# An attention and FFN kernel: batch 0's maximum spread by halves, first scores moved ahead of group 1's transposes, FFN constants made on Pool

## The reference

```python
ig = (ifg @ igate_w.T + igate_b).T          # ifg = [q, k, v] side by side
log_f = jax.nn.log_sigmoid(ifg @ fgate_w.T + fgate_b).T
cs = jnp.cumsum(log_f, axis=1)
log_D = where(tril, cs[:, :, None] - cs[:, None, :], -inf) + ig[:, None, :]
max_log_D = jnp.max(log_D, axis=-1, keepdims=True)
C = (qk / sqrt(16)) * exp(log_D - max_log_D)
h = (C / (maximum(abs(C.sum(-1)), exp(-max_log_D)) + 1e-6)) @ v
x = x + layernorm(h) * ln_scale
```

## Time and profile before

| | |
|---|---|
| median of 3 runs | 128.93 us (128.54 to 129.97) |
| profiled execution: its own time | 127.34 us |
| profiled execution: span | 125.6 us |
| PE matmuls, busy share of the span | 84% |
| DVE | 82% |
| ACT | 62% |
| POOL | 49% |
| mean granted TensorE clock | 0.973 of full |

### The profile page before, as it was taken

The page is one execution under the profiler, slowest core; times in us unless marked ns, Lnnn a source line. Parts: engine busy times, 40 slices in busy tenths (PEclk is TensorE's granted clock), DMA queues, the critical chain, the costliest instruction groups (busy, mean ns, idle before and its releaser), DMA issues.

```text
span 125.6 us, 3302 instructions
## 1 busy us (share of the span) xinstructions
PE 105.5 (84%) x1087; PEld 74.8 (60%) x1087; DVE 103.0 (82%) x347; ACT 78.1 (62%) x226; POOL 62.1 (49%) x137
## 2 busy tenths in 40 slices
PE   4889797928974578999979999999999999898950
PEld 4777793513451234468655866766866767696940
DVE  5459968999969999983999799999899999847331
ACT  4012939982984969478867996988897342525110
POOL 6835040527687857845363665864751554520000
PEclk9999999999999955999999999999999999999999
DMA  2995134982873259600311990100100100110101
GB/s 69 257 242 123 32 65 163 240 198 94 300 281 67 45 198 266 211 0 3 55 31 44 343 337 14 44 5 0 42 0 0 47 0 0 52 42 0 42 5 42
DMA packets 13537, 12.56 MB, mean 100 GB/s; under 512 B 2112, under 2 KB 11728, under 8 KB 13520
## 3 DMA queue, kind: packets, MB, share of 16 engines
q1 hardware_dynamic: 12384, 12.00, 33.2%
q10 hardware_dynamic: 1136, 0.35, 1.1%
HBM read 9.99 MB, written 1.31 MB: 90 GB/s over the span
## 4 chain that ended last, share of the span: by engine, by line
POOL 37%; issue 27%; PE 10%; DMA 8%; DVE 7%; ACT 4%; SPq 4%; POOLq 1%; DVEq 0%; ACTq 0%
POOL maxb L941 9%; POOL rs_x L910 7%; POOL rs_h L910 6%; PE pF L438 6%; POOL x2p L960 5%; SPq L292 4%; DMA xs<-in_x 3%; DMA maxb<-running_max 3%; POOL ve_x L909 2%; POOL ve_h L909 2%; PE pF L417 2%; POOL vals L931 2%; DMA running_max<-max_row 2%; POOL rs_q L920 2%; ACT dmat L550 2%
## 5 line engine op out<-in xcount | busy, mean ns | idle before, releaser
L550 ACT ACTIVATE dmat<-maxb,aT 128x128 f32<-128x128 f32 x128 | 39.2, 391 | 0.4 <-DVE maxb L685 0.4
L438 PE MATMUL pF<-h,w 128*128 128x256 f16 x256 | 30.3, 273 | 0.0
L438 PEld LDWEIGHTS pF<-h,w 128*128 128x128 f16 x256 | 24.7, 98 | 2.6
L790 DVE SCALAR_TENSOR_TENSOR h<-pF,h 128x512 f16<-128x512 f32 x32 | 20.9, 679 | 5.9 <-ACT h L573 5.9
L573 ACT ACTIVATE h<-pF 128x512 f16<-128x512 f32 x32 | 18.0, 591 | 9.8 <-PE pF L438 9.8
L368 PE MATMUL pS<-q_heads,qcT 64*128 64x512 f32 x64 | 20.4, 662 | 1.8 <-DVE cmat L696 1.8
L696 DVE SCALAR_TENSOR_TENSOR cmat<-pS,dmat 128x512 f32<-128x512 f32 x32 | 20.4, 680 | 0.5 <-PE pS L368 0.3
L960 POOL TENSOR_TENSOR x2p<-x,x2p 128x128 f16<-128x128 f32 x16 | 6.8, 427 | 25.3 <-ACT x2p L565 25.3
L941 POOL TENSOR_SCALAR_AFFINE_SELECT maxb<-maxb 128x1024 f32<-128x1024 f32 x14 | 15.4, 1102 | 6.4 <-DMA maxb<-running_max 6.4
L380 PEld LDWEIGHTS pO<-cmat,vals 128*32 128x32 f32 x256 | 6.4, 112 | 11.1 <-issue 9.0
L380 PE MATMUL pO<-cmat,vals 128*32 128x128 f32 x256 | 10.7, 287 | 1.8 <-POOL vals L931 0.9
(11 more groups left out here) (93 smaller groups left out, 170.2 us busy)
## 6 DMA issues: line engine op xcount, KB each, us to landing
maxb<-running_max SPq DMA_DIRECT2D x14, 512.0 KB, 5.9
xs<-in_x SPq DMA_DIRECT2D x4, 256.0 KB, 5.4
q_heads<-qcT SPq DMA_DIRECT2D x32, 32.0 KB, 2.2
out<-outb SPq DMA_DIRECT2D x8, 128.0 KB, 1.8
cs_in<-in_ctx SPq DMA_DIRECT2D x3, 256.0 KB, 6.8
cs_in<-in_ctx ACTq DMA_DIRECT2D x1, 256.0 KB, 4.5
k_in<-in_L_ffn_k SPq DMA_DIRECT2D x1, 256.0 KB, 5.6
running_max<-max_row SPq DMA_DIRECT2D x4, 64.0 KB, 1.7
```

The source lines that it names most:

```text
L438: last = pe.matmul(bank[:, u], w1[:, k, columns], h1[:, k, part], start=(k == 0 and part == 0), stop=(k == FT - 1 and part == 1))
L550: last = act.activation(dmat[:, n % 2, h], maxb[:, g % 2, j, h], ACT.Exp, bias=aT[:, g % 2, j, h:h + 1], scale=-1.0)
L790: dve.scalar_tensor_tensor(out=hidden(f, m, 1), in0=ffn_place(f, m), scalar=0.0, in1=hidden(f, m, 0), op0=ALU.max, op1=ALU.subtract).then_ ...
```

## The change

- `spread_max` and `direct_mask` work by half batches, with a semaphore count for each half, and batch 1's halves go to a third FFN bank and to `pO`, no longer to `pS`. ACT's `decay` of batches 0 and 1 waits for its own half. `scores(0)` no longer waits for the masks.
- PE: `scores(0)` now stands ahead of `turn(1, 1)` and `turn(1, 0)`.
- ACT: both halves of `decay(0)` stand ahead of `turn_out(1, 1)`. `gate_out` signals after each of its reads, and the addition of EPS (`em_guard`) is a function of its own behind `turn_out(1, 0)`.
- `ffn_scalars` goes from DVE to Pool, between `q_scale(0, 4)` and `q_scale(4, 4)`. `ffn_weights_0_2` goes to Pool too, behind `take_values(1)` and a wait for `m_ready`; it has four instructions there instead of three, through a new tile.
- DVE: the four half masks stand ahead of `q_group(2)`; in slot 0 `norm_group(2)` stands ahead of `forget_min(1)`, and `gate_scans(1)` stands behind `make_c(1)` in slot 1.

The diff, without the two functions removed from DVE, which are the same but for w0 (there `w0 = k0_in[0] - k0_in[1]`, then times the scale in place):

```diff
@@ -122,6 +122,7 @@
         k0_in = sb("k0_in", [128, 2, F], U8)
         k1_in = sb("k1_in", [128, FT, F], U8)
         k2_in = sb("k2_in", [128, FT, D], U8)
+        w0_half = sb("w0_half", [128, 2, F], F16)
         w0 = sb("w0", [128, F], F16)
         w1 = sb("w1", [128, FT, F], F16)
         w2 = sb("w2", [128, FT, D], F16)
@@ -205,6 +206,8 @@
         max_ready = sem("max_ready")
         m_ready = sem("m_ready")
         am_turned = sem("am_turned")
+        aT_ready = sem("aT_ready")
+        am_taken = sem("am_taken")
         am_ready = sem("am_ready")
         max_stored = sem("max_stored")
         max_spread = [[sem(f"max_spread{p}{j}") for j in range(GB)] for p in range(2)]
@@ -248,9 +251,9 @@
 
         def direct_place(i, half):
 
-            if i == 1:
-                return pS[:, 4 * half:4 * half + 4]
-            return pF[half][:, :].rearrange("p a (h s) -> p (a h) s", s=S)
+            if (i, half) == (1, 1):
+                return pO[:, :]
+            return pF[2 * i + half][:, :].rearrange("p a (h s) -> p (a h) s", s=S)
 
         def hidden(f, m, part):
 
@@ -320,7 +323,7 @@
                 if part == 1:
                     pe.wait_ge(ctx_loaded[g], 16)
                     if g >= 1:
-                        pe.wait_ge(am_ready, g)
+                        pe.wait_ge(am_taken, g)
                 else:
                     pe.wait_ge(xn_ready, GB * (g + 1))
                     pe.wait_ge(turned_out, 2 * g + 1)
@@ -344,14 +347,13 @@
                 pe.transpose(pG[:, 2], a_row[:, :], ident[:, :])
                 pe.transpose(pG[:, 3], m_row[:, :], ident[:, :]).then_inc(am_turned, 1)
 
-            def spread_max(i):
-
+            def spread_max(i, half):
 
                 g, j = divmod(DIRECT[i], GB)
                 pe.wait_ge(max_ready, g + 1)
-                for h in range(NH):
+                for h in range(4 * half, 4 * half + 4):
                     row = 32 * j + h
-                    last = pe.matmul(direct_place(i, h // 4)[:, h % 4], ident[:, row:row + 1].broadcast_to([128, 128]),
+                    last = pe.matmul(direct_place(i, half)[:, h % 4], ident[:, row:row + 1].broadcast_to([128, 128]),
                                      max_row[:, g % 2], start=True, stop=True)
                 last.then_inc(direct_spread, 1)
 
@@ -359,8 +361,6 @@
                 g, j = divmod(n, GB)
                 if j == 0:
                     pe.wait_ge(heads_spread[g % 2], 16 * NH * (g // 2 + 1))
-                if n == 0:
-                    pe.wait_ge(direct_masked, 2)
                 for half in range(2):
                     if n >= 1:
                         pe.wait_ge(c_ready, 2 * (n - 1) + half + 1)
@@ -462,12 +462,14 @@
             keep_busy(2)
             gates(0)
             keep_busy(10)
-            spread_max(0)
+            spread_max(0, 0)
             turn_am(0)
-            spread_max(1)
+            spread_max(0, 1)
+            spread_max(1, 0)
+            spread_max(1, 1)
+            scores(0)
             turn(1, 1)
             turn(1, 0)
-            scores(0)
             gates(1)
             for n in range(SLOTS):
                 g, k = divmod(n, GB)
@@ -524,25 +526,30 @@
                 act.activation(w1[:, :, :], k1_in[:, :, :], ACT.Identity, bias=s_work[:, 6:7],
                                scale=s_work[:, 5:6]).then_inc(w1_ready, 1)
 
+            def em_row(g):
+                return em[:, g % 2].rearrange("p j h -> p (j h)")
+
             def gate_out(g):
                 act.wait_ge(am_turned, g + 1)
                 if g >= 2:
                     act.wait_ge(o_read, GB * (g - 1))
-                act.copy(aT[:, g % 2].rearrange("p j h -> p (j h)"), pG[:, 2])
-                e = em[:, g % 2].rearrange("p j h -> p (j h)")
-                step(act.activation(e, pG[:, 3], ACT.Exp, scale=-1.0))
-                act.activation(e, e, ACT.Copy, bias=EPS).then_inc(am_ready, 1)
+                act.copy(aT[:, g % 2].rearrange("p j h -> p (j h)"), pG[:, 2]).then_inc(aT_ready, 1)
+                act.activation(em_row(g), pG[:, 3], ACT.Exp, scale=-1.0).then_inc(am_taken, 1)
+
+            def em_guard(g):
+                act.wait_ge(am_taken, g + 1)
+                act.activation(em_row(g), em_row(g), ACT.Copy, bias=EPS).then_inc(am_ready, 1)
 
             def decay(n, heads):
 
                 if n >= B:
                     return
                 g, j = divmod(n, GB)
+                if n in DIRECT:
+                    act.wait_ge(direct_masked, 2 * DIRECT.index(n) + heads[-1] // 4 + 1)
                 if heads[0] == 0:
-                    act.wait_ge(am_ready, g + 1)
-                    if n in DIRECT:
-                        act.wait_ge(direct_masked, DIRECT.index(n) + 1)
-                    else:
+                    act.wait_ge(aT_ready, g + 1)
+                    if n not in DIRECT:
                         act.wait_ge(masked, masked_to(n))
                     if n >= 2:
                         act.wait_ge(c_ready, 2 * (n - 1))
@@ -586,9 +593,10 @@
             ffn_weights_1()
             gate_out(0)
             decay(0, range(NH // 2))
+            decay(0, range(NH // 2, NH))
             turn_out(1, 1)
-            decay(0, range(NH // 2, NH))
             turn_out(1, 0)
+            em_guard(0)
             for n in range(SLOTS):
                 g, k = divmod(n, GB)
                 prepare = n < B and g + 1 < NG
@@ -598,6 +606,7 @@
                     gate_logs(g + 1)
                 if prepare and k == 1 and g > 0:
                     gate_out(g + 1)
+                    em_guard(g + 1)
                 if n == 1:
                     take_o(0)
                 if k == 3 and g + 2 < NG:
@@ -608,6 +617,7 @@
                     turn_out(g + 2, 0)
                 if n == 2:
                     gate_out(1)
+                    em_guard(1)
                 decay(n + 1, range(NH))
                 for f, m in ffn_of_slot(n)[0]:
                     high(f, m)
@@ -676,15 +686,13 @@
                 dve.wait_ge(max_ready, g + 1)
                 dve.tensor_tensor(m_row[:, :], cumf[:, :], max_row[:, g % 2], ALU.add).then_inc(m_ready, 1)
 
-            def direct_mask(i):
+            def direct_mask(i, half):
 
                 g, j = divmod(DIRECT[i], GB)
-                dve.wait_ge(direct_spread, i + 1)
+                dve.wait_ge(direct_spread, 2 * i + half + 1)
                 dve.wait_ge(consts_ready, 1)
-                for half in range(2):
-                    last = dve.tensor_tensor(maxb[:, g % 2, j, 4 * half:4 * half + 4], direct_place(i, half),
-                                             above[:, :].unsqueeze(1).broadcast_to([128, 4, S]), ALU.max)
-                last.then_inc(direct_masked, 1)
+                dve.tensor_tensor(maxb[:, g % 2, j, 4 * half:4 * half + 4], direct_place(i, half),
+                                  above[:, :].unsqueeze(1).broadcast_to([128, 4, S]), ALU.max).then_inc(direct_masked, 1)
 
             def make_c(n):
                 dve.wait_ge(exp_ready, n + 1)
...
@@ -840,14 +826,14 @@
             step(dve.tensor_copy(wkv[:, :, 0:NH], gate_cols(1)))
             dve.tensor_tensor(wkv[:, :, 0:NH], gate_cols(2), wkv[:, :, 0:NH], ALU.add).then_inc(gatew_ready, 1)
             q_group(1)
-            ffn_scalars()
             forget_min(0)
             norm_group(1)
             gate_scans(0)
+            direct_mask(0, 0)
+            direct_mask(0, 1)
+            direct_mask(1, 0)
+            direct_mask(1, 1)
             q_group(2)
-            direct_mask(0)
-            direct_mask(1)
-            ffn_weights_0_2()
             for n in range(SLOTS):
                 g, k = divmod(n, GB)
                 prepare = n < B and g + 1 < NG
@@ -861,8 +847,9 @@
                 if n < B:
                     make_c(n)
                 if n == 0:
+                    norm_group(2)
                     forget_min(1)
-                    norm_group(2)
+                if n == 1:
                     gate_scans(1)
                 if prepare and k == 0 and n > 0:
                     gate_scans(g + 1)
@@ -959,6 +946,29 @@
                 pool.wait_ge(x2_high, n + 1)
                 pool.tensor_tensor(x2p[:, n % 2, 1], x2[:, n % 2], x2p[:, n % 2, 0], ALU.subtract).then_inc(x2_low, 1)
 
+            def ffn_scalars():
+
+                pool.wait_ge(ffns_loaded, 16 * 3)
+                step(pool.tensor_scalar(s_work[:, 0:2], s_in[:, 0:2], 0.0, 2.0, ALU.is_ge, ALU.mult))
+                step(pool.tensor_scalar(s_work[:, 0:2], s_work[:, 0:2], 1.0, None, ALU.subtract))
+                step(pool.tensor_tensor(s_work[:, 2:4], s_work[:, 0:2], s_in[:, 0:2], ALU.mult))
+                step(pool.tensor_scalar(s_work[:, 4:5], s_work[:, 0:1], W0_SCALE, None, ALU.mult))
+                step(pool.tensor_scalar(s_work[:, 5:6], s_work[:, 1:2], 2.0 * W1_SCALE, None, ALU.mult))
+                step(pool.tensor_scalar(s_work[:, 6:7], s_work[:, 1:2], -W1_SCALE, None, ALU.mult))
```

(34 more changed lines are left out.)

## The result

The changed kernel takes 131.91 us (median of 4 runs, 131.31 to 132.49) against 128.74 us for the kernel before (4 runs, 128.08 to 129.97): ratio 1.0235, 95% interval 1.0139 to 1.033. A second measurement gave 131.49 us and a ratio of 1.0146 (1.0073 to 1.0218). It is slower by 2.4 to 3.2 us; the forecast was 131.3 us, +2.4. The profiled execution took 132.49 us with a span of 130.6; the mean granted clock was 0.922.

What follows compares the result with a forecast made beforehand. Group 1's maximum, through ACT's copy, SyncE's queue, two DMAs and Pool, was taken to set the start of DVE's saturated stretch; scan +2.2, copy +3.0, store's end +2.4, put on the median 128.93, gave 131.3 us, range 129.4 to 133.4.

Steps and rivals of the forecast that it cites:

- Scalars on Pool: Nine scalar instructions ahead of `q_scale(4, 4)` on Pool, 10.4 to 13.1, move the first scan from 13.57 to 15.8, +2.2 us.
- the sum: All terms of the ramp together: +2.4 us on the median 128.93, giving 131.3 us; chance 0.50.
- Spread: PE's spreading products keep 3.89 us, 17.1 to 21.0; with `scores(0)` ahead, group 1's last transposes copy ends at 24.75, +3.0.
- the first rival: PE's longer gap before the spread drops TensorE's clock to 1.2 GHz: +1.4 us more, 132.7 us; chance 0.22.
- Store and loads: Store of group 1's maximum waits for SyncE's queue (29.9) and second `max_row`, starts 30.2, takes 1.7: +2.4 us.
- Pool sets the residual: DVE's residual of batch 1 still waits for Pool's `rs_h`, moving +2.4 us; DVE's own work, +2.25, stays covered.
- What was costed at nothing: Masks, later `q_group(2)`, weights on Pool (1.0 to 4.4 us) and DVE's relief were taken as hidden, adding no time.
- Faster: Rival: DVE was the bound and, relieved of 3.45 us, keeps what the late norm leaves: -1.25, 127.7 us; chance 0.12.
- Early scalars: Rival: the third scalar DMA lands at 8.9, the scan slips 0.7 instead of 2.2, 129.8 us; chance 0.16.

Runs made afterwards that it cites:

- the one moved line: Changed kernel with the nine scalar instructions still on Pool but behind `q_scale(4, 4)` instead of ahead of it: 129.38 us, ratio 0.9978 to the kernel before.
- scores behind: Changed kernel with `scores(0)` behind group 1's transposes again, all else as changed: 131.08 us, ratio 1.0138 to the kernel before.
- runs with fillers: Extra PE filler products: 22 for 10 in the changed kernel (129.92 us); four in slots 1 to 4, scalars behind `q_scale(4, 4)` (129.86) or on DVE (128.64).
- the halves alone: Changed kernel with scalars on DVE, `scores(0)` behind the transposes and group 1's scans in slot 0: 129.8 us, beside 129.42 of before.

## Why the prediction was right, step by step

**Scalars on Pool: right mechanism, the landing mis-sized.** They were to begin at 10.4; they began at 11.86 in the first profile of the changed kernel and at 10.65 in the second, 9.7 at the earliest of all. The nine take 2.67 us (forecast 2.7). In the second profile `max_row` ends at 17.08, forecast 17.05. Most of the delay is those 2.67 us on Pool, as the sum had it; the wait for the DMA adds 0.2 and 1.1 us in the two profiles. That the nine ahead of the reciprocal are what costs is shown by the one moved line (1.0146 to 0.9978) and by the scalars back on DVE (0.9909).

**Spread: the sum left the clock out, and it fell.** 3.89 us was taken, 5.42 and 5.6 were measured; that was the first rival, with 0.22. It had put the time at 132.7, the sum at 131.3; the medians of 131.5 and 131.9 lie between, so the time alone doesn't tell them apart, and the profiles do: the half clock is there. The copy of the last transposes ended at about 26.3 and 27.7, not 24.75.

**Store and loads: right in form.** The two conditions were named and the later one counts; the scan was it in every run of the new order. The store took 1.57 to 1.59 us (forecast 1.7). The 2.58 of the earlier trace rows was of that execution: in the second profile of the kernel before it took 1.81. With the clock it began at 31.79 in the second profile, not 30.2.

**Pool sets the residual: right for the changed kernel's two profiles, not in general.** There DVE waits 1.14 us for `rs_h` as before. In the second profile of the kernel before, and in those of the scores behind and of only the scalars moved, DVE had waited 1.31 to 1.50 us for PE at 1.2 GHz instead. The residual's start by the profiles, with the time of the same execution:

| kernel | its time | residual of batch 1 starts | time less start |
|---|---|---|---|
| before | 127.34 | 37.37 | 89.97 |
| before, second | 129.91 | 38.95 | 90.96 |
| changed | 132.49 | 42.54 | 89.95 |
| changed, second | 130.96 | 41.31 | 89.65 |
| scalars on DVE | 129.2 | 38.49 | 90.7 |

In these five the rest behind it is the same within 1.3 us; over all fourteen profiles it runs from 88.4 to 91.0, and the two lowest are runs with fillers. So a shift of the ramp does go to the end, but single pairs of executions carry up to 2.6 us of something else.

**Why the sum came out although the clock fell.** In part by luck: two errors met. From the lucky profile of before to the second of the changed kernel the residual moves by 3.9 us, 1.5 more than summed, which is the size of the clock's part in the products (5.42 less 3.89). But a usual execution of the kernel before has its own fall at 28 to 38 us, and starts that residual 1.6 us later, while neither profile of the changed kernel has a fall between 22 and 44 us. Between this one and the changed kernel's second it is 41.31 - 38.95 = 2.4, the forecast's number; but the times of these two differ by only 1.05 us, and with the changed kernel's first profile it would be 3.6, so the agreement of that pair proves little. The medians (+2.4 and +3.2) bear the forecast out. I had put the difference on the median, and had not asked why the median lies 1.6 us above the profiled execution.

**What was costed at nothing.** The weights on Pool were bounded by 4.4 us and took 6.5: two instructions from uint8 take 1.58 us each, and the one for `w2` 1.93. In the changed kernel they stay hidden, since the statistics for `q_scale(8, 4)` came at 25.9 and the weights were done at 25.2; with the scalars out of the way they do hold DVE, by 1.3 us with the scalars on DVE and 1.87 in the run with the moved line. The place of the scores was costed at 1.1 us on the copy, which is about right, and measured as nothing on the time. The move of group 1's scans was counted only as a condition for the store; undoing it cost 1.2 us or more, so it gains, through `make_c(1)`.

**The other rivals.** Faster didn't come, but its mechanism, DVE relieved, may be what remains once the late norm is mended (0.9909, by the medians 0.997); that it is DVE's relief, no run shows by itself. Early scalars weren't shown: in no profile did work on them begin before 9.7.

## What to carry to other kernels

Before moving small work to an idle engine, look at what it waits for and what stands behind it there: here nine small instructions of 2.7 us, put ahead of a reciprocal that the critical scan needs, cost 2 to 3 us, of which the wait for their DMA made at most 1.1, and one line further down the loss was gone. Where two conditions gate a store, gaining on the earlier one is worth nothing. And where one profiled execution lies 1.6 us below the median, take a second profile before summing on it.

## What the runs showed of the hardware that was not expected

TensorE's clock in the spread. In six profiled executions PE stood idle for 2.05 to 3.17 us ahead of these products (the changed kernel twice, scores behind, only the scalars moved, the halves alone, the scalars' DMAs early), and in all six the granted clock fell to 1.2 GHz within 0.9 us of their start: 5.4 to 5.6 us for the 32 records. In the other eight the gap was 0 to 1.50 us, and they ran at 2.4 GHz: 3.9 to 4.1 us. So the penalty is paid by the work behind the gap, not in it. The Trainium skill (TensorE: Matmul & The Clock Gate, "What's actually happening") has the clock set by how busy the engine has recently been; by that, these traces agree.

A DMA of 0.5 KB is no quick one among 256 KB loads: each of the three scalars landed 4.2 to 8.1 us after its issue, the last of them between 9.6 and 11.9 us of the span in these profiles, and one issue alone took 1.74 us of ACT's queue in the first profile of the changed kernel.

GpSimd on uint8: 128x512 to f16 took 1.58 us in a multiplication by a column and 1.93 in a two-step multiply and subtract, where VectorE needed 0.43 for the latter; two f16 inputs took 1.16. The nine tiny instructions took 2.67 us on Pool and 1.59 on DVE, 1.7 times as long; the Trainium skill (GPSIMD Engine Reference, section 3.1) has 1.96 for an addition of 2048 columns, so for tiny ones the ratio measured here is the lower one.

VectorE beside GpSimd: the residual of batch 1 (128x128 f32) took 0.34 us in six of the fourteen profiles and 1.09 in eight, and in all eight it began 0.15 us behind the start of Pool's mask of 1.10 us. In the six it began 0.08 us behind that mask's end, and the operation ahead of it (0.34 alone as well) took 0.39 to 1.28 us, until about the same end. So in these traces VectorE seems held until Pool's mask ends; no run tests it.
